# A cross-attention and expert-layer kernel: a new order for the prologue's instructions, 15 identity transposes in its gaps, and a last copy in two pieces

## The chip, the cores and the metric

One core of one Trainium2 chip runs the whole program. The metric is the device time of one launch in microseconds (us), as the median of several runs. "Faster" means less of it.

## What is computed

16 batches of 100 rows of width 256 go through two residual blocks. Cut to what matters:

```python
LN = layernorm                       # over the 256 columns, no weight
# block 1: 16 heads of width 16, keys and values from ctx (16, 361, 256)
Q, K, V = LN(x) @ Wq.T + bq, ctx @ Wk.T + bk, ctx @ Wv.T + bv
p   = softmax(Q K^T / 4)             # per batch and head: 100 x 361
x   = x + tanh(g_xattn) * ((p V) @ Wh.T + bh)
# block 2: 8 experts as low-rank deltas on shared weights, the best 2 per row
t   = rmsnorm(LN(x)) * norm_w
w   = top-2 of softmax(t @ gate_w.T), scaled to sum 1
h1  = t @ w1.T + 2 (t a1_e^T) b1_e^T ;  h3 the same with w3, a3, b3
o_e = (silu(h1) h3) @ w2.T + 2 (...) ;  x = x + tanh(g_ffn) * sum_e w_e o_e
```

## The kernel before

All five engines run one hand-written instruction list each, and semaphores tie them together. A wait on an engine holds back everything behind it on that engine, so the written order is the schedule. There are four stages.

**The prologue** (0 to 44.18 us here). TensorE first does 34 transposes of the 128x128 identity, which depend on nothing but `ident`. Then, for four chunks c of four batches each, the rows are normalized, turned and projected to queries; keys and values of batches 0 and 1 are made; and the 16 score heads of batch 0 are run for their row maxima. The steps, with their function and line:

- `stat`, `spread_of` (L786 to L795), `shift_of` (L799): mean and variance of the batches, on VectorE; `rooted` (L538): the root, on ScalarE.
- `normed` (ScalarE, L533): four batches of one chunk normalized into `xn`. `normed(2)` is batches 8 to 11, `normed(3)` batches 12 to 15.
- `turn(n)` (TensorE, L1216): batches 2n and 2n+1 transposed; `turned(n)` (ScalarE, L475) copies them out of PSUM into `xnT`.
- `q_proj(c, j)` (TensorE, L1227): half j of the queries of chunk c, in bank 2 or 3. `q_high` (ScalarE, L484) and `q_low` (VectorE, L809) split it into a high and a low part; after `q_low` the bank is free.
- `k_proj(b, j)` (L1240), then `k_high` (ScalarE, L496) and `k_low` (VectorE, L818); `v_proj(b, t)` (L1252), then `v_out` (ScalarE, L502).
- `s_head(b, h)` (TensorE, L1270): score head h of batch b, in bank 0 or 1 by turns; `head(b, h)` (VectorE, L985) takes its row maxima. A score head waits for the maxima of the head two before it, which leave its bank.
- `row_turn(0, half)` (TensorE, L1276) turns the maxima of eight heads, and `row_copy`, `row_send` (ScalarE, L513, L517) put them beside the queries.

The queries and keys are stacked for the scores by DMA: `kn` to `KS` from SyncE (`k_stack`, L244, high parts) and GpSimd (`k_stack_low`, L343, low parts), and `q_dram` to `QS` from SyncE (L259) and GpSimd (L363 for batch 0, `q_load`, L333 for later ones). GpSimd also computes the low part of the context (`ctx_low`, L328) and loads later contexts (`ctx_load`, L338).

**The attention body** (`body(i)`, from 44.18 us on): for each batch the exponentials and products with V, together with the scores of the next batch and the keys and values of the one after. Before the first `body`, TensorE waits for `q_low` of the last chunk (`pe.wait_ge(m["q_l"], KT * NC + KT)`), since `st_unit` (L1293) writes the same banks 2 and 3.

**The expert stage**: 32 steps over 4 chunks and 8 slices of the inner width.

**The end**: `down_low` (L1514) finishes the two halves of the output of the last chunk in banks 0 and 1; `out_half` copies one by ScalarE (L632) and the other by VectorE (L950, 128x400); `out_turn_last` (L1503, L1507) transposes both, four pieces each; `added` (L955) adds them to `xs`, two batches at a time; SyncE stores them (L304).

Of the kernel before, what the change touches and what calls it, by code (L numbers as in the profile page):

```python
# [21 lines left out]
KT = D // 128  # L22
# [19 lines left out]
def program(nc, x, ctxT, g_x, g_f, wqT, bq, wkT, bk, wvT, bv, whT, bh,  # L42
            norm_w, w1T, w3T, w2T, agT, b1T, b3T, a2T, b2T, out):
    es = ExitStack()
    with es:
# [263 lines left out]
        def _(pool):  # L309
# [9 lines left out]
            def low_w(w):  # L319
                pool.wait_ge(m["wkv_h"], w + 1)  # L320
                nc.gpsimd.tensor_tensor(wkv[:, w, 1], wst[:, w], wkv[:, w, 0].bitcast(F32), ALU.subtract).then_inc(m["wkv_l"], 1)

            def ctx_low(b):
                if b == 1:
                    pool.wait_ge(m["ctx_ha"], 1)
                else:
                    pool.wait_ge(m["ctx_h"], b if b else 1)
                nc.gpsimd.tensor_tensor(cth[:, b % 2, 1], craw[:, b % 2], cth[:, b % 2, 0].bitcast(F32), ALU.subtract).then_inc(m["ctx_l"], 1)  # L328
# [7 lines left out]
            def ctx_load(b):  # L336
                wait(pool, "ctx_l", b - 1)
                pool.dma_start(craw[:, b % 2, :, 0:T], ctxT[b]).then_inc(ctx_sw[b % 2], 16)  # L338

            def k_stack_low(b):  # L340
                pool.wait_ge(m["dve_kl"], KT * b + KT)
                for g in range(4):
                    pool.dma_start(KS[b % 3][64:96, g, :, :].rearrange("p j t -> p (j t)").bitcast(F32),  # L343
                                   kn[32 * g:32 * g + 32, b % 2, 1, :, :].rearrange("p j t -> p (j t)").bitcast(F32)).then_inc(klst[b % 3][g], 16)

# [10 lines left out]
            ctx_low(0)  # L356
            low_w(0)
            low_w(1)
            pool.wait_ge(m["zero"], 3)
            pool.wait_ge(q_first, 32)  # L360
            src = q_dram[1].rearrange("(g o p) c s -> o p g c s", g=4, o=2)
            for odd in range(2):
                pool.dma_start(QS[0][32 + DH * odd:32 + DH * odd + DH, :, odd, :, :].rearrange("p g j s -> p g (j s)").bitcast(F32),  # L363
                               src[odd][:, :, 0, 0:KT * S]).then_inc(qst[0], 16)
            k_stack_low(0)
            ctx_low(1)
            ctx_load(2)

            def body(i):
# [81 lines left out]
        def _(act):  # L451
# [21 lines left out]
            def turned(n):  # L473
                act.wait_ge(m["xnT_t"], n + 1)
                nc.scalar.activation(xnT[:, :, 2 * n * S:2 * (n + 1) * S].rearrange("p k (b s) -> p b k s", b=2),  # L475
                                     (pT[2], pO)[n % 2][:, 0:2 * KT * S].rearrange("p (b k s) -> p b k s", b=2, k=KT),
                                     ACT.Copy).then_inc(m["xnT_ok"], 1)

            def q_high(c, j):
                act.wait_ge(m["q_mm"], c * KT + j + 1)  # L480
                wait(act, q_out[c % 2], 32 * (c // 2))
                if c == 2:
                    act.wait_ge(q_first, 32)
                nc.scalar.activation(qn[:, c % 2, 0, :, j, :], pT[j][:, 0:CS].rearrange("p (b s) -> p b s", b=4), ACT.Identity, bias=bqs[:, j:j + 1]).then_inc(m["q_h"], 1)  # L484
# [6 lines left out]
            def k_high(b, j):  # L491
                act.wait_ge(m["pe_k"], KT * b + j + 1)
                if j == 0 and b > 1:
                    for g in range(4):
                        wait(act, kst[(b - 2) % 3][g], stacked(32, b - 2, (b - 2) % 3))
                nc.scalar.activation(kn[:, b % 2, 0, j, :], pP[(1, 0)[j]][:, 0:TP], ACT.Identity,  # L496
                                     bias=bks[:, j:j + 1]).then_inc(m["act_kh"], 1)

            def v_out(b, t):
                bank = (pS[0], pS[1], pT[2])[t] if b == 0 else pP[1] if b == 1 and t == 1 else pP[0]  # L500
                act.wait_ge(m["pe_v"], NT * b + t + 1)
                nc.scalar.activation(va[0:TW[t], b % 3, t, :, 0:DH],  # L502
                                     bank[0:TW[t], 0:D].rearrange("p (h d) -> p h d", h=H),
                                     ACT.Copy).then_inc(m["act_v"], 1)
# [20 lines left out]
                nc.scalar.activation(pt[0:TW[t], u, :], pT[u % 3][0:TW[t], 0:CS], ACT.Exp,  # L525
                                     scale=float(DH) ** -0.5).then_inc(m["act_e"], 1)

            def normed(c):
                act.wait_ge(m["xnT_t"], 2 * c - 2)
                act.wait_ge(m["nmr_ok"], 3)  # L530
                act.wait_ge(m["xn_ok"], 6)
                for b in range(4 * c, 4 * c + 4):
                    nc.scalar.activation(xn[:, b % 8, :], xs[:, b, :], ACT.Identity, bias=nmr[:, b:b + 1],  # L533
                                         scale=rstd[:, b:b + 1]).then_inc(m["xn_ok"], 1)

# [26 lines left out]
            q_high(1, 1)  # L562
            rooted(2, 8, B)
            k_high(1, 0)
            k_high(1, 1)
            normed(2)
            turned(4)
            turned(5)
            q_high(2, 0)
            row_out(0, 0)  # L570
            q_high(2, 1)
            v_out(1, 0)
            normed(3)
            v_out(1, 1)
            turned(6)
            turned(7)
            nc.scalar.activation(warm_e[:], nmr[:, 0:1], ACT.Exp).then_inc(m["exp_ok"], 1)
            q_high(3, 0)
            q_high(3, 1)
# [187 lines left out]
        def _(dve):  # L767
# [211 lines left out]
            def head(b, h):  # L979
                n = b * H + h  # L980
                dve.wait_ge(m["pe_s"], n + 1)
                if h % 8 == 0:
                    wait(dve, "pe_cT", 2 * b - 1 + h // 8)
                pos = h // 4 * 4 + h % 2 * 2 + h % 4 // 2
                nc.vector.tensor_reduce(nmax[:, h // 8, pos % 8:pos % 8 + 1], pS[h % 2][0:S, 0:T], AX.X, ALU.max, negate=True).then_inc(m["dve_s"], 1)  # L985
# [24 lines left out]
            stat(2)  # L1010
            stat(3)
            q_low(1, 0)
            q_low(1, 1)
            head(0, 0)
            head(0, 1)
            spread_of(2, 8, B)
            head(0, 2)
            head(0, 3)
            shift_of(2, 8, B)
            k_low(1, 0)  # L1020
            head(0, 4)
            head(0, 5)
            k_low(1, 1)
            head(0, 6)
            head(0, 7)
            q_low(2, 0)
            head(0, 8)
            q_low(2, 1)
            head(0, 9)
            ctx_high(2)  # L1030
            head(0, 10)
            head(0, 11)
            head(0, 12)
            q_low(3, 0)
            head(0, 13)
            q_low(3, 1)
            head(0, 14)
            head(0, 15)

            def body(i):  # L1040
                b = i + 2
# [152 lines left out]
            dve.wait_ge(m["d_zt"], 2 * NC)  # L1194
            dve.wait_ge(m["pe_b2"], 2 * (NC - 1))
            nc.vector.tensor_tensor(zm[:], zt[:, 0], zt[:, 1], ALU.add).then_inc(m["d_zm"], 1)
            out_half(NC - 1)
            added(NC - 1, 0)
            added(NC - 1, 1)

# [2 lines left out]
        def _(pe):  # L1203
# [80 lines left out]
            def st_unit(b, u):  # L1284
                n = b * UN + u
                q, t = u // NT, u % NT
                if u == 0:
                    wait(pe, "cr_a", 16 * (b + 1))
                if u == UN // 2:
                    wait(pe, "cr_b", 16 * (b + 1))  # L1290
                wait(pe, "act_e", n - 2)
                for j in range(KT):
                    last = mm(pT[u % 3][0:TW[t], j * 2 * S:(j + 1) * 2 * S],  # L1293
                              KS[b % 3][:, q, j, T0[t]:T0[t] + TW[t]],
                              QS[b % 3][:, q, :, j, :], start=True, stop=True)
                last.then_inc(m["pe_st"], 1)
# [202 lines left out]
            def out_turn_last():  # L1499
                pe.wait_ge(m["d_wb"], 2 * NC)  # L1500
                pe.wait_ge(m["a_fo"], NC)
                for k in range(4):
                    nc.tensor.transpose(ps[6 + k // 2][0:S, k % 2 * D:k % 2 * D + 128], fo[:, 0, k * S:(k + 1) * S], ident[:])  # L1503
                pe.wait_ge(m["d_fo"], NC)
                for k in range(4):
                    col = k % 2 * D + 128
                    last = nc.tensor.transpose(ps[6 + k // 2][0:S, col:col + 128], fo[:, 1, k * S:(k + 1) * S], ident[:])  # L1507
                    if k % 2:
                        last.then_inc(m["pe_out"], 1)
# [6 lines left out]
            def out_turn(c):  # L1516
# [3 lines left out]
                for k in range(4):  # L1520
# [3 lines left out]
                    if k % 2:  # L1524
                        last.then_inc(m["pe_out"], 1)

            for _ in range(34):
                nc.tensor.transpose(pP[0][:, 0:128], ident[:], ident[:])
            turn(0)
# [14 lines left out]
            s_head(0, 1)  # L1544
            pe.wait_ge(m["dve_kl"], 1)
            k_proj(1, 0)
            s_head(0, 2)
            s_head(0, 3)
            pe.wait_ge(m["dve_kl"], 2)
            k_proj(1, 1)  # L1550
            s_head(0, 4)
            s_head(0, 5)
            s_head(0, 6)
            turn(4)
            turn(5)
            s_head(0, 7)
            q_proj(2, 0)
            s_head(0, 8)
            pe.wait_ge(m["dve_kl"], 3)
# [3 lines left out]
            pe.wait_ge(m["dve_kl"], 4)  # L1563
            v_proj(1, 0)
            s_head(0, 10)
            s_head(0, 11)
            pe.wait_ge(m["act_c"], 1)
            v_proj(1, 1)
            s_head(0, 12)
            turn(6)  # L1570
            turn(7)
            q_proj(3, 0)
            s_head(0, 13)
            q_proj(3, 1)
# [3 lines left out]
            s_head(0, 15)  # L1578
            pe.wait_ge(ones_in, 32)
            pe.wait_ge(m["xnT_ok"], 2 * NC)  # L1580
            pe.wait_ge(m["q_l"], KT * NC + KT)

            def body(i):
                b = i + 2
# [221 lines left out]
```

## Time and profile before

| what | value |
|---|---|
| median of 3 runs | 499.56 us (498.75 to 500.44) |
| the profiled execution, its own time | 499.88 us |
| span of its instructions | 498.0 us |
| TensorE busy | 482.1 us (97%) |
| VectorE, ScalarE, GpSimd busy | 358.4, 265.7, 276.9 us |
| mean granted TensorE clock | 0.995 |

### The profile page before, as it was taken

The numbers are of one execution on the slowest core, as the hardware profiler recorded it, in microseconds if no ns is written. First come the engines' busy times: TensorE is split into PE (matmuls) and PEld (weight loads), VectorE is DVE, ScalarE is ACT, GpSimd is POOL, SyncE is SP. The second block draws the span as 40 slices with busy tenths as digits, with TensorE's granted clock in tenths as the row PEclk, the third lists the DMA queues.
The fourth block names the chain that finished last, engine by engine and source line by source line (L and its number), as shares of the span: only waits on it lengthen the run. The fifth ranks groups of instructions, "written<-read, shape, count | busy, mean of one in ns | idle before, by whom it ended". The sixth has DMA issues, their size and how long they took to land.

```text
span 498.0 us, 11753 instructions
## 1 busy us (share of the span) xinstructions
PE 482.1 (97%) x4350; PEld 454.2 (91%) x4350; DVE 358.4 (72%) x771; ACT 265.7 (53%) x584; POOL 276.9 (56%) x336
## 2 busy tenths in 40 slices
PE   7888999999999999999999999999999999999996
PEld 6657999999999999998999998899999999999994
DVE  5866787888888888988797779745585566764444
ACT  4466766666777766669865532533325333333331
POOL 6545665666666677685434547544485435845440
PEclk9989999999999999999999999999999999999999
DMA  7693786678777676554260000010000100001001
GB/s 214 176 291 98 219 208 163 153 183 195 199 184 180 174 188 158 121 111 79 50 185 1 1 0 2 1 34 1 0 2 0 34 1 1 0 2 34 0 1 33
DMA packets 51144, 45.83 MB, mean 92 GB/s; under 512 B 33935, under 2 KB 40115, under 8 KB 51088
## 3 DMA queue, kind: packets, MB, share of 16 engines
q1 hardware_dynamic: 41310, 23.18, 19.8%
q0 software_dynamic: 7504, 18.69, 14.0%
q10 hardware_dynamic: 2274, 3.21, 2.0%
q8 instruction: 35, 0.57, 0.5%
q14 instruction: 21, 0.17, 0.1%
HBM read 20.59 MB, written 6.66 MB: 55 GB/s over the span
## 4 chain that ended last, share of the span: by engine, by line
PE 90%; DVE 5%; DMA 2%; issue 1%; ACT 1%; SPq 0%; DVEq 0%; ACTq 0%
PE bank L1426 14%; PE bank L1270 9%; PE bank L1293 8%; PE bank L1306 7%; PE bank L1430 7%; PE bank L1443 7%; PE bank L1478 6%; PE bank L1252 6%; PE bank L1240 6%; PE bank L1458 4%; PE bank L1339 3%; PE bank L1461 2%; PE bank L1227 2%; DMA xs<-x 2%; PE bank L1386 2%; PE bank L1318 1%
## 5 line engine op out<-in xcount | busy, mean ns | idle before, releaser
L985 DVE TENSOR_REDUCE nmax<-bank 100x1 f32<-100x361 f32 x256 | 131.1, 530 | 34.0 <-PE bank L1270 29.7
L419 POOL TENSOR_TENSOR awl<-hb,awh 128x400 fp32r<-128x400 f32 x63 | 71.4, 1134 | 119.5 <-ACT awh L623 119.5
L623 ACT ACTIVATE awh<-hb 128x400 fp32r<-128x400 f32 x64 | 34.5, 538 | 118.4 <-DVE hb L921 118.1
L525 ACT ACTIVATE pt<-bank 120x400 f32<-120x400 f32 (+1 forms) x192 | 90.1, 501 | 12.6 <-PE bank L1293 9.5
L1270 PE MATMUL bank<-KS,QS 96*100 96x362 f32 x256 | 86.3, 357 | 3.7 <-DVE nmax L985 2.9
L914 DVE TENSOR_TENSOR hb<-sil,bank 128x400 f32<-128x400 f32 x64 | 36.4, 569 | 71.2 <-PE bank L1443 36.7
L1293 PE MATMUL bank<-QS,KS 97*120 97x200 f32 (+1 forms) x384 | 63.6, 269 | 0.0
L328 POOL TENSOR_TENSOR cth<-craw,cth 128x724 fp32r<-128x724 f32 x16 | 27.7, 1730 | 59.9 <-ACT cth L471 53.6
L1293 PEld LDWEIGHTS bank<-QS,KS 97*120 97x120 f32 (+1 forms) x384 | 59.2, 184 | 0.2
L1270 PEld LDWEIGHTS bank<-KS,QS 96*100 96x100 f32 x256 | 41.6, 167 | 9.6 <-DVE nmax L985 3.3
L333 POOL DMA_DIRECT2D QS<-q_dram x90 | 46.1, 521 | 0.4 <-issue 0.3
L1252 PE MATMUL bank<-wkv,cth 128*120 128x256 f32 (+1 forms) x288 | 45.2, 286 | 0.0
L921 DVE TENSOR_TENSOR hb<-hb,wbT 128x400 f32<-128x400 f32 x64 | 43.4, 678 | 2.1
L1240 PE MATMUL bank<-cth,wkv 128*128 128x362 f32 x192 | 42.0, 331 | 0.0
L343 POOL DMA_DIRECT2D KS<-kn x64 | 31.9, 508 | 15.1 <-DVE kn L818 9.7
L618 ACT ACTIVATE sil<-bank 128x400 f32<-128x400 f32 x64 | 31.6, 493 | 16.3 <-PE bank L1430 11.7
L1252 PEld LDWEIGHTS bank<-wkv,cth 128*120 128x120 f32 (+1 forms) x288 | 39.3, 183 | 0.3 <-issue 0.3
L1306 PE MATMUL bank<-pt,va 120*17 120x100 f32 (+1 forms) x1536 | 36.5, 249 | 0.0
L1306 PEld LDWEIGHTS bank<-pt,va 120*17 120x17 f32 (+1 forms) x1536 | 32.5, 97 | 3.9 <-issue 3.6
L423 POOL TENSOR_TENSOR awsl<-aws,awsh 128x400 fp32r<-128x400 f32 x31 | 34.0, 1097 | 0.0
L1240 PEld LDWEIGHTS bank<-cth,wkv 128*128 128x128 f32 x192 | 32.7, 190 | 0.3
L513 ACT ACTIVATE crow<-bank 8x100 fp32r<-8x100 f32 x32 | 7.7, 242 | 31.4 <-PE bank L1276 31.4
(225 smaller groups left out, 1117.1 us busy)
## 6 DMA issues: line engine op xcount, KB each, us to landing
KS<-kn SPq DMA_DIRECT2D x128, 90.5 KB, 3.3
KS<-kn POOLq DMA_DIRECT2D x64, 90.5 KB, 3.5
craw<-ctxT POOLq DMA_DIRECT2D x14, 361.0 KB, 5.0
QS<-q_dram POOLq DMA_DIRECT2D x92, 50.0 KB, 3.3
q_dram<-qn ACTq DMA_DIRECT2D x4, 400.0 KB, 4.4
o_dram<-on SPq DMA_DIRECT2D x16, 100.0 KB
xr<-o_dram SPq DMA_DIRECT2D x16, 100.0 KB
y<-xs SPq DMA_DIRECT2D x8, 200.0 KB
```

Of the source, the lines that this page charges most:

```text
L333: pool.dma_start(QS[b % 3][row + DH * odd:row + DH * odd + DH, :, odd, :, :].rearrange("p g j s -> p g (j s)").bitcast(F32), src[odd]).the ...
L419: nc.gpsimd.tensor_tensor(awl[:, g % 2, slot], hb[:, slot], awh[:, g % 2, slot].bitcast(F32), ALU.subtract).then_inc(m["p_awl"], 1)
L525: nc.scalar.activation(pt[0:TW[t], u, :], pT[u % 3][0:TW[t], 0:CS], ACT.Exp, scale=float(DH) ** -0.5).then_inc(m["act_e"], 1)
L914: nc.vector.tensor_tensor(hb[:, slot], sil[:, slot], pU[1][:, 0:CS], ALU.mult).then_inc(m["d_hb"], 1)
L921: nc.vector.tensor_tensor(hb[:, slot], hb[:, slot], wbT[g // FT % 2][:, slot], ALU.mult).then_inc(m["d_aw"], 1)
L985: nc.vector.tensor_reduce(nmax[:, h // 8, pos % 8:pos % 8 + 1], pS[h % 2][0:S, 0:T], AX.X, ALU.max, negate=True).then_inc(m["dve_s"], 1)
L1240: last = mm(pP[(1, 0)[j]][:, 0:TP], wkv[:, 0, hw, k, j * 128:(j + 1) * 128], cth[:, b % 2, hc, k, :], start=p == 0, stop=p == 5)
L1252: last = mm(bank[0:TW[t], 0:D], cth[:, b % 2, hc, k, T0[t]:T0[t] + TW[t]], wkv[:, 1, hw, k, :], start=p == 0, stop=p == 5)
L1270: mm(pS[h % 2][0:S, 0:TP], QS[b % 3][0:96, g, h % 2, j, :], KS[b % 3][0:96, g, j, :], start=True, stop=True).then_inc(m["pe_s"], 1)
L1293: last = mm(pT[u % 3][0:TW[t], j * 2 * S:(j + 1) * 2 * S], KS[b % 3][:, q, j, T0[t]:T0[t] + TW[t]], QS[b % 3][:, q, :, j, :], start=True, ...
L1306: last = mm(pO[32 * g:32 * g + VW, q * S:(q + 1) * S], va[0:TW[t], b % 3, t, 4 * q + g, :], pt[0:TW[t], u, g * S:(g + 1) * S], start=t == ...
L1426: mm(pU[a][:, 0:CS], up_w[a][hw][:, j, fs], tt[hc][c % 2][:, j, :], start=t + j == 0, stop=False)
```

## The change

On TensorE, 15 further transposes of the identity into bank 2 are placed in the prologue, in groups of 2, 4, 2, 2, 2 and 3, each group behind a wait for `q_low(1, *)` (`keep_warm`). `turn(4)` stands before score head 6 instead of behind it and `turn(5)` behind head 7 instead of before it; `turn(6)`, `turn(7)` go from behind head 12 to ahead of `v_proj(1, 1)`, and head 11 goes behind that. The wait for the last `q_low` leaves the end of the prologue and is split over the first two `st_unit`. On VectorE, `head(0, 0)` goes ahead of `q_low(1, 1)`, `shift_of(2, ...)` ahead of `head(0, 3)`, `k_low(1, 1)` behind `head(0, 6)`, `ctx_high(2)` behind `head(0, 12)`, and the two `q_low(3, *)` one and two heads later. On ScalarE, `normed(2)` comes before `k_high(1, 1)`, three of the four steps of `normed(3)` before `q_high(2, 0)` and the fourth before `v_out(1, 0)`, and `v_out(1, 1)` behind `turned(7)`. On GpSimd, two of the four `k_stack_low(0)` transfers go ahead of the query load, the other two behind `ctx_low(1)`. At the end, VectorE's copy is made in two pieces of 200 columns, and the transposes wait for one piece each.

```diff
@@ gpsimd @@
+            k_stack_low(0, 0, 2)
             pool.wait_ge(m["zero"], 3)
             pool.wait_ge(q_first, 32)
...
-            k_stack_low(0)
             ctx_low(1)
+            k_stack_low(0, 2, 4)
             ctx_load(2)
@@ scalar @@
             k_high(1, 0)
+            normed(2, 0, 4)
             k_high(1, 1)
-            normed(2)
             turned(4)
             turned(5)
+            normed(3, 0, 3)
             q_high(2, 0)
             row_out(0, 0)
             q_high(2, 1)
+            normed(3, 3, 4)
             v_out(1, 0)
-            normed(3)
-            v_out(1, 1)
             turned(6)
             turned(7)
+            v_out(1, 1)
@@ vector @@
             q_low(1, 0)
+            head(0, 0)
             q_low(1, 1)
-            head(0, 0)
             head(0, 1)
             spread_of(2, 8, B)
             head(0, 2)
+            shift_of(2, 8, B)
             head(0, 3)
-            shift_of(2, 8, B)
...
             dve.wait_ge(m["pe_b2"], 2 * (NC - 1))
             nc.vector.tensor_tensor(zm[:], zt[:, 0], zt[:, 1], ALU.add).then_inc(m["d_zm"], 1)
-            out_half(NC - 1)
+            dve.wait_ge(m["pe_b2"], 2 * NC)
+            for pair in range(2):
+                cs = slice(pair * 2 * S, (pair + 1) * 2 * S)
+                nc.vector.tensor_copy(fo[:, 1, cs], pY[1][:, cs]).then_inc(m["d_fo"], 1)
@@ tensor, st_unit @@
+                if b == 0 and u < KT:
+                    pe.wait_ge(m["q_l"], KT * NC + KT - 1 + u)
@@ tensor, out_turn_last @@
-                pe.wait_ge(m["d_fo"], NC)
                 for k in range(4):
+                    if k % 2 == 0:
+                        pe.wait_ge(m["d_fo"], NC + k // 2)
@@ tensor, prologue @@
+            def keep_warm(n):
+                pe.wait_ge(m["q_l"], 3 * KT)
+                for _ in range(n):
+                    nc.tensor.transpose(pT[0][:, 0:128], ident[:], ident[:])
...
             pe.wait_ge(ones_in, 32)
             pe.wait_ge(m["xnT_ok"], 2 * NC)
-            pe.wait_ge(m["q_l"], KT * NC + KT)
```

TensorE, from score head 4 of batch 0 (bank 0) to the first projection of chunk 2 (bank 2 from `xnT,wq`); before:

```order
L1270 MATMUL bank0<-KS0,QS0 100x362
L1270 MATMUL bank1<-KS0,QS0 100x362
L1270 MATMUL bank0<-KS0,QS0 100x362
L1216 MATMUL bank4<-ident,xn 128x100 x4
L1216 MATMUL bank5<-ident,xn 128x100 x4
L1270 MATMUL bank1<-KS0,QS0 100x362
L1227 MATMUL bank2<-xnT,wq 128x400 x2
```

The same place in the changed kernel, whose lines are some numbers further down:

```order
L1275 MATMUL bank0<-KS0,QS0 100x362
L1538 MATMUL bank2<-ident 128x128 x4
L1275 MATMUL bank1<-KS0,QS0 100x362
L1538 MATMUL bank2<-ident 128x128 x2
L1221 MATMUL bank4<-ident,xn 128x100 x4
L1275 MATMUL bank0<-KS0,QS0 100x362
L1538 MATMUL bank2<-ident 128x128 x2
L1275 MATMUL bank1<-KS0,QS0 100x362
L1538 MATMUL bank2<-ident 128x128 x2
L1221 MATMUL bank5<-ident,xn 128x100 x4
L1538 MATMUL bank2<-ident 128x128 x3
L1232 MATMUL bank2<-xnT,wq 128x400 x2
```

Thirteen of the 15 identity transposes stand here, and the turn into bank 4 has gone ahead of a score head; the work between the first and the last row is otherwise the same.

TensorE again, from the first value projection of batch 1 (bank 6) to the first projection of chunk 3; before:

```order
L1252 MATMUL bank6<-wkv,cth 121x256 x6
L1270 MATMUL bank0<-KS0,QS0 100x362
L1270 MATMUL bank1<-KS0,QS0 100x362
L1252 MATMUL bank7<-wkv,cth 120x256 x6
L1270 MATMUL bank0<-KS0,QS0 100x362
L1216 MATMUL bank4<-ident,xn 128x100 x4
L1216 MATMUL bank5<-ident,xn 128x100 x4
L1227 MATMUL bank2<-xnT,wq 128x400 x2
```

and in the changed kernel:

```order
L1257 MATMUL bank6<-wkv,cth 121x256 x6
L1275 MATMUL bank0<-KS0,QS0 100x362
L1221 MATMUL bank4<-ident,xn 128x100 x4
L1221 MATMUL bank5<-ident,xn 128x100 x4
L1257 MATMUL bank7<-wkv,cth 120x256 x6
L1275 MATMUL bank1<-KS0,QS0 100x362
L1275 MATMUL bank0<-KS0,QS0 100x362
L1232 MATMUL bank2<-xnT,wq 128x400 x2
```

Both turns moved up by a value projection and two score heads; head 11 (bank 1) now has the turns and the projection ahead of it.

VectorE, from head 12 to head 15 of batch 0 and head 0 of batch 1 (the last two `TENSOR_REDUCE`); before:

```order
L985 TENSOR_REDUCE nmax<-bank0 100x1
L809 SCALAR_TENSOR_TENSOR qn<-bank2,bqs,qn 128x4x100
L985 TENSOR_REDUCE nmax<-bank1 100x1
L809 SCALAR_TENSOR_TENSOR qn<-bank3,bqs,qn 128x4x100
L985 TENSOR_REDUCE nmax<-bank0 100x1
L985 TENSOR_REDUCE nmax<-bank1 100x1
L985 TENSOR_REDUCE nmax<-bank0 100x1
```

and in the changed kernel:

```order
L987 TENSOR_REDUCE nmax<-bank0 100x1
L781 CAST cth<-craw 128x724
L987 TENSOR_REDUCE nmax<-bank1 100x1
L811 SCALAR_TENSOR_TENSOR qn<-bank2,bqs,qn 128x4x100
L987 TENSOR_REDUCE nmax<-bank0 100x1
L987 TENSOR_REDUCE nmax<-bank1 100x1
L811 SCALAR_TENSOR_TENSOR qn<-bank3,bqs,qn 128x4x100
L987 TENSOR_REDUCE nmax<-bank0 100x1
```

Each `q_low` of chunk 3 moved down past one or two heads, the second past all that is left of batch 0, and the cast of context 2 now stands behind head 12.

## Rows read from the trace of the kernel before

**Rows 1.** Busy time by stretch: from:to, length, engines in order, granted clock, DMA share, GB/s.

```profile
7.20:10.00 2.80, 0.94 (x9) 0.78 (x9) 1.44 (x4) 2.27 (x6) 1.05 (x1) 1.00 0.92 282
...
25.60:29.00 3.40, 2.22 (x13) 1.38 (x12) 2.95 (x8) 3.14 (x8) 0.56 (x2) 1.00 1.02 338
29.00:32.40 3.40, 2.92 (x6) 1.48 (x6) 0.53 (x1) 0.48 (x1) 3.40 (x7) 0.50 1.04 372
...
44.20:490.00 445.80, 443.91 (x4161) 426.56 (x4162) 327.02 (x683) 242.44 (x537) 248.75 (x292) 1.00 0.33 81
```

**Rows 2.** The chain of waits, 26 to 45 us: start, length (us), what.

```profile
26.37 1.97 ACT xn L533 x4
...
29.58 3.00 PE bank L1227 x4
32.58 0.17 PE bank L1270
32.75 0.09 PE bank L1276
32.84 1.38 PE bank L1227 x4
...
36.02 0.41 PE bank L1270
36.43 0.72 PE bank L1252 x6
...
37.38 0.71 PE bank L1216 x8
38.09 0.67 issue
38.76 1.58 PE bank L1227 x4
...
44.18 0.25 PE bank L1276
```

**Rows 3.** Instructions in order of time: start, length, engine, line, idle before it.

```profile
17.66 1.21 POOL L363 DMA_DIRECT2D QS<-q_dram  x2 [4.53 <-DMA q_dram<-qn]
18.86 2.00 POOL L343 DMA_DIRECT2D KS<-kn  x4
...
22.77 0.55 PE L1270 MATMUL bank<-KS,QS 96*100 96x362 f32 x2 [0.72 <-DMA KS<-kn]
...
28.98 0.50 ACT L475 ACTIVATE xnT<-bank 128x400 f32<-128x400 f32 x1 [0.26 <-PE bank L1216]
...
34.92 0.33 PE L1270 MATMUL bank<-KS,QS 96*100 96x362 f32 x1
...
42.57 0.33 PE L1270 MATMUL bank<-KS,QS 96*100 96x362 f32 x1
```

**Rows 4.** The opening transposes (L1528) alone, by stretch: length, TensorE, weight loads.

```profile
1.50:2.50 1.00, 0.97 (x5) 0.97 (x6) 1.00 0.48 76
...
6.00:6.50 0.50, 0.50 (x7) 0.50 (x6) 1.00 0.84 256
```

**Rows 5.** VectorE's groups by shape, 12 to 24 us: count, busy us, mean ns, idle.

```profile
L809 DVE SCALAR_TENSOR_TENSOR qn<-bank,bqs,qn 128x400 fp32r<-128x400 f32 x2 | 1.3, 634 | 1.5 <-ACT qn L484 1.5
...
L985 DVE TENSOR_REDUCE nmax<-bank 100x1 f32<-100x361 f32 x2 | 1.0, 524 | 0.0
L809 DVE SCALAR_TENSOR_TENSOR qn<-bank,bqs,qn 128x100 fp32r<-128x100 f32 x2 | 0.6, 300 | 0.0
```

**Rows 6.** ScalarE's groups by shape, 12 to 44 us.

```profile
L484 ACT ACTIVATE qn<-bank,bqs 128x400 fp32r<-128x400 f32 x8 | 4.8, 595 | 8.4 <-PE bank L1227 8.4
```

**Rows 7.** The last query load for batch 1 (L333), issued at 33.0 us.

```profile
DMA to landing us min/median/max: 5.0/5.0/5.0
```

**Rows 8.** The end, in order of time, columns as in rows 3.

```profile
492.26 0.57 DVE L950 COPY fo<-bank 128x400 f32<-128x400 f32 x1 [1.70 <-PE bank L1514]
...
493.36 1.41 DVE L955 SCALAR_TENSOR_TENSOR xs<-bank,tgf,xs 100x512 f32<-100x512 f32 x2 [0.52 <-PE bank L1507]
```

More of the change, by code:

```diff
@@ L338, in ctx_load, with k_stack_low @@
                 pool.dma_start(craw[:, b % 2, :, 0:T], ctxT[b]).then_inc(ctx_sw[b % 2], 16)
-            def k_stack_low(b):
+            def k_stack_low(b, g0=0, g1=4):
                 pool.wait_ge(m["dve_kl"], KT * b + KT)
-                for g in range(4):
+                for g in range(g0, g1):
                     pool.dma_start(KS[b % 3][64:96, g, :, :].rearrange("p j t -> p (j t)").bitcast(F32),
@@ L526, in expo, with normed @@
                                      scale=float(DH) ** -0.5).then_inc(m["act_e"], 1)
-            def normed(c):
+            def normed(c, k0, k1):
                 act.wait_ge(m["xnT_t"], 2 * c - 2)
@@ L531, in normed @@
                 act.wait_ge(m["xn_ok"], 6)
-                for b in range(4 * c, 4 * c + 4):
+                for b in range(4 * c + k0, 4 * c + k1):
                     nc.scalar.activation(xn[:, b % 8, :], xs[:, b, :], ACT.Identity, bias=nmr[:, b:b + 1],
@@ L1022, in _ @@
             head(0, 5)
+            head(0, 6)
             k_low(1, 1)
-            head(0, 6)
             head(0, 7)
@@ L1029, in _ @@
             head(0, 9)
-            ctx_high(2)
             head(0, 10)
@@ L1033, in _ @@
             head(0, 12)
+            ctx_high(2)
+            head(0, 13)
             q_low(3, 0)
-            head(0, 13)
-            q_low(3, 1)
             head(0, 14)
             head(0, 15)
+            q_low(3, 1)
             def body(i):
@@ L1546, in _ @@
             k_proj(1, 0)
+            keep_warm(2)
             s_head(0, 2)
@@ L1551, in _ @@
             s_head(0, 4)
+            keep_warm(4)
             s_head(0, 5)
+            keep_warm(2)
+            turn(4)
             s_head(0, 6)
-            turn(4)
+            keep_warm(2)
+            s_head(0, 7)
+            keep_warm(2)
             turn(5)
-            s_head(0, 7)
+            keep_warm(3)
             q_proj(2, 0)
@@ L1565, in _ @@
             s_head(0, 10)
-            s_head(0, 11)
+            turn(6)
+            turn(7)
             pe.wait_ge(m["act_c"], 1)
             v_proj(1, 1)
+            s_head(0, 11)
             s_head(0, 12)
-            turn(6)
-            turn(7)
             q_proj(3, 0)
```

## The prediction

> **What bounds the kernel now.** I read the busy time by stretch first. From 44.20 to 490.00 us TensorE is busy for 443.91 of 445.80 us [rows 1], so whatever lets the attention body start earlier moves all that follows by as much, and only the prologue and the last few microseconds have anything to give. The point to watch is the second `row_turn` of batch 0, at 44.18 us [rows 2]: from there on the order of work is the old one.
>
> The chain of waits shows what the prologue waits for. TensorE is not the cause up to 29.48 us: four normalizations (26.37 us, 1.97 long), then `turn(5)`, then `turned(5)` on ScalarE, which ends at 28.98 + 0.50 = 29.48 [rows 2, 3]. Behind it stand four losses, all on TensorE's path:
>
> - **The clock.** From 29.00 to 32.40 us the granted clock is 0.50, that is 1.2 GHz [rows 1]. `q_proj(2, 0)` takes 3.00 us there, and the same work at 38.76 us takes 1.58 at 2.4 GHz [rows 2]: 1.42 us lost. In the 3.40 us before the fall TensorE was busy for 2.22 [rows 1].
> - **Head 11.** Head 10 ends at 34.92 + 0.33 = 35.25 [rows 3]. Head 11 waits for the maxima of head 9, which stand behind `q_low(2, 1)` on VectorE, and ends at 36.43 [rows 2]. A head in a dense stream takes 0.17 [rows 2]. Lost: 36.43 - 35.25 - 0.17 = 1.01 us.
> - **`q_proj(3, 0)`.** `turn(7)` ends at 38.09; the projection waits for `turned(7)` and ends at 38.76 + 1.58 = 40.34 [rows 2]. Without a gap it takes 1.38, as `q_proj(2, 1)` does [rows 2]. Lost: 40.34 - 38.09 - 1.38 = 0.87 us.
> - **The last heads.** Head 15 ends at 42.57 + 0.33 = 42.90 [rows 3], and the `row_turn` comes 1.28 us later, since head 14's maxima stand behind `q_low(3, 1)`.
>
> **The change, part by part.**
>
> *Up to 29.5 us: 0.* The first score head started after 0.72 us of idling for a `KS` transfer that GpSimd issued at 18.86, behind two query loads. GpSimd had idled for 4.53 us before these [rows 3], so two key transfers (a half of the 2.00) fit there and the query loads are not held up. The head may start some 0.7 us earlier, but the chain goes through ScalarE, not through it. There `normed(2)` begins one `k_high` earlier, and that `k_high` then stands ahead of `turned(4)`; the two cancel, and `q_proj(2, 0)` starts at 29.5 again. What this makes late: the keys of batch 1 leave two microseconds later on SyncE and one later on GpSimd (rival 3).
>
> *The identity transposes: their own cost 0, the clock -1.4.* At the end of the opening run 7 of them take 0.50 us [rows 4], 0.071 each, so 15 take 1.07. Thirteen fall between heads 4 and `q_proj(2, 0)`, 13 x 0.071 = 0.92, in gaps in which TensorE waits for maxima and normalizations: 3.40 - 2.22 = 1.18 us are idle there [rows 1]. If a gap were gone, the group in it would cost at most 4 x 0.07 = 0.3. They raise the busy time of that stretch from 2.22 to about 3.1 of 3.40. I take the full 1.42 as gained. Against: between 7.20 and 10.00 TensorE was busy for only 0.94 of 2.80 and the clock stayed at 1.00 [rows 1], so busy time alone does not tell when it falls. Bounds: 0 and 1.42.
>
> Do such transposes count as work for the clock at all? At the start nothing else ran on TensorE: 5 of them in the first microsecond, then 7 in a half [rows 4], and the pace more than doubled. I read this as the clock rising on transposes alone, though the column of the granted clock says 1.00 throughout. The Trainium skill says the opposite ("TensorE: Matmul & The Clock Gate", Part 4: PE-mode transpose): transposes do not count as work in the same way, and the full clock does not engage for them. By that rule the 15 do nothing and the sum below is smaller by its clock term. The trace speaks against the rule, so it is a rival and not the forecast.
>
> *The order behind 29.5 us: -2.6.* TensorE's list now has `turn(6)`, `turn(7)` and `v_proj(1, 1)` ahead of head 11. I lay it out densely. `q_proj(2, 0)`, head 8, `row_turn` and `q_proj(2, 1)`: 29.5 + 1.58 + 0.17 + 0.09 + 1.38 = 32.72. Then up to head 15 seven heads (7 x 0.17), three value projections (3 x 0.72), two turns (0.71) and two query projections (2 x 1.38): 6.82, which makes 39.54 [rows 2]. Is any of it held? Head 12 needs the maxima of head 10: 32.72 plus `q_high` 0.60, `q_low` 0.63 and two maxima of 0.52 is 35.0 [rows 5, 6], and TensorE comes there at 35.4. `q_proj(3, 0)` needs `turned(7)`, which has a value projection and two heads to run beside, 1.06 us, more than the 0.67 it was waited for [rows 2]. So the losses of 1.01 and 0.87 go. At the end, `q_low(3, 1)` stands behind head 15 and TensorE no longer waits for it before `row_turn`; what is left is the maxima of head 15, 0.52 and some hundredths, so 1.28 becomes 0.56 and -0.72 comes out. The `row_turn` falls at 39.54 + 0.56 = 40.1 instead of 44.18: -4.08, of which 1.42 is the clock and -2.66 the order (1.01 + 0.87 + 0.72 and 0.06 of rounding). Against it: `q_low(3, 1)`, 0.63, now stands ahead of the maxima of head 0 of batch 1, for which head 2 waits. They end 0.63 + 0.52 = 1.15 behind `row_turn`, where head 2 would be issued at about 1.0: +0.15. Together -3.95. Lower bound of the order's part: if head 11's hold and the one at the end come back whole in other places, -0.8; upper bound -2.66.
>
> *The copy in two pieces: -0.25.* It takes 0.57 for 400 columns [rows 8]. `q_low` at 400 and 100 columns takes 634 and 300 ns [rows 5], 1.11 ns a column, so 200 columns fewer save 0.22 and a piece takes 0.35. The transposes of the first pair start that much earlier, the second piece (0.35) runs beside them, and `added` for the second pair follows the first as before. Gain 0.2 to 0.25; the loss can be no more than the second fixed cost, 0.57 - 0.44 = 0.13, if nothing overlaps. -0.2 here.
>
> **The sum.** 0 - 3.95 - 0.2 = -4.15, against the profiled execution's 499.88: 495.7 us. That execution lies 0.3 above the median of the runs, which have a spread of 1.7; I give 495.6.
>
> **Rivals.**
>
> *1. The clock falls all the same* (or in another place of the prologue). For it: the idle stretch at 7.20 without a fall [rows 1] shows that the clock does not simply follow the busy time of a stretch, so 0.92 us more of it need not hold it. Against: the pace of the opening transposes [rows 4]. It gives back 1.42: 495.7 + 1.42 = 497.1 us. The Trainium skill's rule on transposes, above, would end here too.
>
> *2. The waits only move.* TensorE's dense stream of 10 us behind 29.5 needs VectorE and ScalarE on time at every head; the nearest margin is 0.4 us (head 12). If two or three of the heads are late by half a microsecond each, 1.0 to 1.5 come back, with the clock held: 495.7 + 1.2 = 496.9; with rival 1 as well, 498.3.
>
> *3. The stacks of batch 1 become the bound; slower.* The place is head 0 of batch 1, at about 39.5 now. GpSimd's last query load for it was issued at 33.0 and took 5.0 us [rows 7], so it landed at 38.0, well ahead of its use behind 42.90. Now it is issued 0.9 later (it stands behind `k_stack_low(1)`, which waits for the moved `k_low(1, 1)`) and lands at 38.9. From 39.5 on each microsecond of landing costs one. It cancels the gain of 4.15 only where the load needs 33.9 to 43.7, 9.8 us instead of 5, and is slower by over 1.5 from some 11.3 us. For it: the DMA share is 1.02 and 1.04 from 25.60 to 32.40 [rows 1], and the transfers of `KS` now start later in a full queue. Against: the bytes are the same, and a delay of 1 us cannot make them twice as slow. At 11.3 us: 495.7 + (33.9 + 11.3 - 39.5) = 501.4.
>
> *4. Nothing of size changes*, because the shift is absorbed by a wait early in the body, such as one for maxima behind the added `q_low(3, 1)`; only the end's 0.2 is left: 499.6. Against: the body's busy time above.
>
> **Chances.** Forecast 0.55; rival 1 0.20; rival 2 0.14; rival 3 0.04; rival 4 0.07. A measurement here tells 0.3%, 1.5 us, from no change, so "faster" is below 498.1. Forecast, rival 1 and most of rival 2 lie there: 0.83. Same: the rest of rival 2 and rival 4, 0.12. Slower: 0.05. The range has to leave out 2 in 10 at most: its low end is the sum less half the spread of the runs (0.85), 494.8; its high end takes in rival 1, rival 2 and nearly both together, 498.2.
>
> **What would show it.** Right: granted clock 1.00 in all slices of the prologue; `q_proj(2, 0)` at 29.5 taking about 1.6; head 11 directly behind `v_proj(1, 1)`; no gap ahead of `q_proj(3, 0)`; the `row_turn` of batch 0's second half at about 40.1; `added` 0.2 earlier against its copy's start. Wrong: a clock of 0.50 anywhere behind 7 us, idle time of TensorE of over half a microsecond between 30 and 39 us, a wait of head 0 of batch 1 for a DMA, or a body longer than before between that `row_turn` and the end.

## The result and the profile after

| | before | changed |
|---|---|---|
| median of 4 runs | 500.00 us (498.75 to 500.63) | 494.79 us (494.68 to 496.00) |
| ratio, 95% interval | | 0.9906 (0.9880 to 0.9931) |
| the profiled execution | 499.88 us | 494.78 us |
| its span | 498.0 us | 493.0 us |
| second `row_turn` of batch 0 | 44.18 us | 39.52 us |

In a later series, beside the experiments below, the changed kernel had a median of 496.75 us over 10 runs and before 499.74 over 26: ratio 0.9930 (0.9904 to 0.9957). The change makes the kernel faster by 0.7 to 0.9%.

The same changed kernel is thus 2.0 us slower in the later series. Of the 1.9 us between the spans of the two profiled executions (494.9 and 493.0), 0.58 lie ahead of the second `row_turn` and 1.3 behind it. Behind it TensorE waited for two transfers in the later one, for which it did not wait in the first one, nor in the profiled execution of before:

```profile
PE bank L1337 <- DMA xr<-o_dram: 0.7, 1, 0.7
PE bank L1300 <- DMA QS<-crow: 0.2, 1, 0.2
```

Whether the new order makes such waits more frequent is open: there is one trace of the kernel before. What else slows the later series is not known either; its runs had no more falls of the clock than the first.

The chain of waits of the changed kernel, 19 to 40 us (start, length, what), answers to [rows 2]:

```profile
2.08 9.92 DMA xs<-x
...
19.12 2.92 PE bank L1232 x8
...
28.57 0.31 issue
28.88 1.58 PE bank L1232 x4
30.46 0.16 PE bank L1275
30.62 0.09 PE bank L1281
30.71 1.37 PE bank L1232 x4
...
33.14 0.70 PE bank L1221 x8
33.84 0.73 PE bank L1257 x6
34.57 0.33 PE bank L1275 x2
34.90 1.35 PE bank L1232 x4
...
38.84 0.55 DVE nmax L987
39.38 0.14 issue
39.52 0.25 PE bank L1281
```

From 28.88 to 38.81 us the chain is TensorE's own list without a gap. The projection of chunk 2 takes 1.58 us, heads 11 and 12 follow the value projection directly (0.33 us for the two), and the projection of chunk 3 starts with no wait.

Its busy time by stretch, the same columns as [rows 1]:

```profile
25.60:29.00 3.40, 3.09 (x26) 2.59 (x25) 3.18 (x7) 3.40 (x8) 0.18 (x1) 1.00 0.98 358
29.00:32.40 3.40, 3.40 (x14) 2.14 (x15) 1.08 (x2) 2.23 (x6) 3.40 (x8) 1.00 0.98 335
...
40.20:485.90 445.70, 443.70 (x4160) 426.16 (x4158) 327.16 (x683) 242.17 (x536) 252.55 (x299) 1.00 0.34 82
```

The clock stays at 1.00, that is 2.4 GHz, and the body behind is as dense as it was. The span shrank by 5.0 us: 4.66 by the `row_turn`, 0.22 by the copy at the end (below), and the last 0.1 in between, where single waits differ from execution to execution.

### The profile page after: what moved, and what is told of

Read it like the earlier page. It is cut to its first block, busy times and chain, and to the rows that moved or that the text cites. A ratio compares the mean times of both kernels' runs of the same rounds, so it can differ in the third digit from the quotient of the medians.

```text
span 493.0 us, 11786 instructions
## 1 busy us (share of the span) xinstructions
PE 482.1 (98%) x4365; PEld 456.1 (93%) x4365; DVE 358.6 (73%) x772; ACT 265.5 (54%) x584; POOL 277.0 (56%) x336
## 4 chain that ended last, share of the span: by engine, by line
PE 92%; DVE 4%; DMA 2%; issue 1%; SPq 0%; DVEq 0%; ACT 0%
PE bank L1433 14%; PE bank L1275 9%; PE bank L1300 8%; PE bank L1313 7%; PE bank L1437 7%; PE bank L1450 7%; PE bank L1257 7%; PE bank L1485 6%; PE bank L1245 6%; PE bank L1465 4%; PE bank L1346 3%; PE bank L1468 2%; DMA xs<-x 2%; PE bank L1393 2%; PE bank L1232 2%; PE bank L1325 1%
## 5 line engine op out<-in xcount | busy, mean ns | idle before, releaser
L333 POOL DMA_DIRECT2D QS<-q_dram x90 | 46.1, 521 | 0.4 <-issue 0.2
```

The lines of the kernel that those rows point to most:

```text
L333: pool.dma_start(QS[b % 3][row + DH * odd:row + DH * odd + DH, :, odd, :, :].rearrange("p g j s -> p g (j s)").bitcast(F32), src[odd]).the ...
```

## How the experiments are read

Executions differ ahead of the part in question. The first transfers land at other times: in some the chain starts with the rows (`DMA xs<-x`, as above), in others with the first context, and then the query projections of chunk 1 end up to 1.3 us later; in three (no opening transposes, turns late, a step further) it starts with a fill of `KS` by VectorE. So positions are counted from the end of these eight records, the **anchor** (19.12 + 2.92 = 22.04 above). "Stream" is the start of the first projection of chunk 2, "turn" the second `row_turn` of batch 0.

| kernel | anchor | to stream | stream to turn | anchor to turn |
|---|---|---|---|---|
| before | 22.06 | 7.52 | 14.60 | 22.12 |
| changed | 22.04 | 6.84 | 10.64 | 17.48 |
| changed, again | 22.63 | 6.82 | 10.65 | 17.47 |
| no transposes | 22.74 | 6.89 | 10.63 | 17.52 |
| no transposes, again | 23.17 | 7.12 | 10.63 | 17.75 |
| transposes alone | 22.06 | 7.53 | 13.17 | 20.70 |
| late half alone | 22.57 | 7.70 | 12.31 | 20.01 |
| no opening transposes | 24.31 | 6.83 | 10.63 | 17.46 |
| turns late | 22.18 | 6.83 | 12.55 | 19.38 |
| GpSimd as before | 22.93 | 7.33 | 10.64 | 17.97 |
| ScalarE as before | 22.79 | 7.26 | 10.64 | 17.90 |
| last wait as before | 22.04 | 6.82 | 11.21 | 18.03 |

An anchor-to-stream time can differ by 0.2 us without a cause in the edit: it is 6.89 and 7.12 in two executions of the kernel without transposes.

Each run also lists its mean granted clock. A fall of 3.4 us to half costs 0.0034 of it over this span, so I count runs with 0.996 or less as runs with a fall. The count is not sharp at 0.997: a fall alone would read 0.9966, and so can a run without one, since the granted clock also drops behind TensorE's last work (the profiled execution of "ScalarE as before" reads 0.997 with 1.00 in all of the prologue, and 0.64 from 490 us on). The runs were taken in series, each on another chip, and the fall is not equally frequent in them, so only kernels of one series are compared:

| series | before | late half alone, no transposes | changed, without the 15 transposes | kernels with the 15 transposes |
|---|---|---|---|---|
| first: the clock, turns late | 15 of 21 | | 0 of 4 | 0 of 26 |
| second: GpSimd, ScalarE, last wait, a step further | 6 of 7 | | | 0 of 7 |
| later: the kernels taken again, late half alone, one copy | 10 of 26 | 6 of 12 | 3 of 11 | 0 of 11 |

With the four runs of the result, the nine kernels that have the 15 transposes come to 0 of 48, against 31 of 54 of before. Five of the 48 stand at 0.997, and the trace of one of the five has no fall; the other four can't be told.

## Experiments on the clock

**The 15 transposes taken out.**

```diff
             def keep_warm(n):
                 pe.wait_ge(m["q_l"], 3 * KT)
-                for _ in range(n):
-                    nc.tensor.transpose(pT[0][:, 0:128], ident[:], ident[:])
```

> The changed kernel without the 15 identity transposes, everything else in its new order. Theory (the transposes hold the clock, the order alone does not): the granted clock falls to 0.50 for some 3.4 us behind 29 us or nearby, the first projection of chunk 2 takes about 3.0 us instead of 1.58, and the time is 1.4 us above the changed kernel's 494.8, about 496.2. Rival (the new order closes the gaps by itself, the transposes do nothing): clock 1.00 throughout, 494.8.

Measured: 495.70 us (494.77 to 496.56, 4 runs), ratio to before 0.9902 (0.9873 to 0.9931); clock 0.998 or 0.999 in all four. Stream to turn 10.63, as in the changed kernel. By these four runs my theory was wrong. But four are few for an event that also stays out now and then in the kernel before, so I took it again, with more runs of both:

> The changed kernel once more, beside the next ones on the same chip. 494.7 to 495.5, clock 0.998 or more in all runs.

> The changed kernel without its 15 identity transposes, with more runs than the first time, in which the clock had not fallen in any of four. If the new order alone holds the clock: 0.997 or more in all runs and within 0.3 us of the changed kernel. If the transposes hold it and the four were luck: 0.994 to 0.996 in most runs, as in the kernel before, and 1.4 us more.

Measured: 496.75 us with the transposes (495.25 to 497.79, 10 runs, lowest clock 0.997) and 496.87 without (495.53 to 499.70, 11 runs, of which three at 0.994, 0.994 and 0.995). Neither expectation holds as it stands. The fall does come with the new order alone, in 3 of 11 runs. Whether the order makes it rarer is not shown: beside it before had 10 of 26, which 11 runs can't tell from 3, while the 0 of 4 of the first series, against 15 of 21, speak for it. With the transposes it was 0 of 10 in the later series. That is fewer than in before (10 of 26), but against the 3 of 11 it could be chance too; what shows that the transposes hold the clock is the next experiment. On the median they are worth 0.1 us here, which is less than these runs can tell.

**The transposes alone, in the order of before.** Added: `keep_warm` as in the change, with 2, 4, 2, 2, 2 and 3 transposes behind the same steps in the old list.

> The kernel before with the 15 identity transposes in the same gaps and its old order. Theory: the clock stays at 1.00 between 22 and 44 us, and the second row turn of batch 0 comes 1.4 us earlier than 44.18, at about 42.7; time 1.4 us below that of before, 498.4. Rival (by the rule that transposes do not count for the clock): it falls all the same, no change.

Measured: 499.04 us (498.16 to 499.44, 10 runs), ratio 0.9971 (0.9956 to 0.9986), no fall in ten runs, beside 15 in the 21 of before. In the profiled execution anchor and stream stand as before, and behind the stream this changed:

```profile
29.59 1.58 PE bank L1227 x4
31.17 0.17 PE bank L1270
31.34 0.09 PE bank L1276
31.43 1.38 PE bank L1227 x4
...
42.76 0.25 PE bank L1276
```

The turn comes at 42.76 instead of 44.18, by the 1.42 us that the prediction had for the clock. The median moved by 1.1 (500.14 to 499.04), since before only some runs had anything to win: 15 of 21, and 0.71 x 1.42 = 1.0. This speaks against the rival by which transposes do not count.

**Only the late half of the order, without transposes.** The changed kernel with the old order of GpSimd, ScalarE, VectorE and TensorE up to the first projection of chunk 2 and an empty `keep_warm`:

```diff
-            k_stack_low(0, 0, 2)
...
-            k_stack_low(0, 2, 4)
+            k_stack_low(0)
             ctx_low(1)
...
-            normed(2, 0, 4)
             k_high(1, 1)
+            normed(2, 0, 4)
...
-            turn(4)
             s_head(0, 6)
+            turn(4)
+            turn(5)
             s_head(0, 7)
-            turn(5)
```

> No identity transposes, and the order of before on all engines up to the first projection of chunk 2; only the order behind it is new. If the clock falls after the sparse stretch between 25.6 and 29 us, as in the trace of before, it falls here too: clock near 0.995 in most runs, projection of chunk 2 about 3.0 us, and time 0.7 (first half) + 1.4 (clock) above the changed kernel, about 497.1. If the dense stream behind it prevents the fall: 495.7 and clock 0.998.

Measured: 497.54 us (496.21 to 500.84, 12 runs), ratio 0.9947 (0.9918 to 0.9976); six of twelve with a fall. The profiled execution is one of them. By stretch:

```profile
25.60:29.00 3.40, 2.13 (x12) 1.27 (x11) 3.36 (x9) 3.23 (x8) 0.05 (x1) 1.00 1.02 371
30.00:31.00 1.00, 0.73 (x1) 0.46 (x2) 0.21 (x1) 1.00 (x4) 1.00 (x3) 0.66 1.02 405
31.00:32.00 1.00, 1.00 (x3) 0.64 (x2) 0.00 (x0) 0.49 (x1) 1.00 (x3) 0.50 1.00 311
```

and its chain:

```profile
30.27 2.97 PE bank L1231 x4
...
33.70 1.44 PE bank L1231 x4
```

The clock goes to 0.50 after a stretch in which TensorE was busy for 2.13 of 3.40 us, close to the 2.22 of before [rows 1]. Stream to turn is 12.31 here and 10.64 in the changed kernel: the fall costs 1.67 in this execution, 0.25 more than the 1.42 of before. So the difference of the two with a fall, 14.60 - 12.31 = 2.29, is too small for the late half of the order; the two without one, the transposes alone and the changed kernel, give 13.17 - 10.64 = 2.53. The dense order behind the stream does not prevent the fall: 6 of 12, beside 10 of 26 of before. Whether the new order ahead of the stream does is not shown: 3 of 11 against 6 of 12 can be chance.

**No opening transposes.**

```diff
-            for _ in range(34):
-                nc.tensor.transpose(pP[0][:, 0:128], ident[:], ident[:])
```

> The changed kernel without the 34 identity transposes at its start, the only other place where nothing but transposes runs. If transposes raise the clock, the first projections of chunk 0 behind 9.9 us now run at 1.2 GHz, each matmul record about 0.7 us instead of 0.36, and two to four us of the prologue are lost: 497 to 499. If they do not count, nothing changes: 494.8.

Measured: 498.43 us (497.24 to 500.15, 10 runs), ratio 0.9961 (0.9943 to 0.9980). The first work of TensorE in this kernel, then in the changed one, in order of time:

```profile
8.43 1.57 PE L1221 MATMUL bank<-ident,xn 100*128 100x100 f32 x8 [8.43 <-DVE xn L806]
10.68 4.48 PE L1232 MATMUL bank<-xnT,wq 128*128 128x400 f32 x8 [0.69 <-ACT xnT L476]
```

```profile
8.34 0.92 PE L1221 MATMUL bank<-ident,xn 100*128 100x100 f32 x8
9.98 2.92 PE L1232 MATMUL bank<-xnT,wq 128*128 128x400 f32 x8 [0.72 <-ACT xnT L476]
```

The same eight records take 4.48 us against 2.92, and the eight transposes ahead of them 1.57 against 0.92, though nothing but transposes was taken away. The first of the eight records last 874 ns each and the last 499, which is the median of all eight in the changed kernel: here the clock rises in the middle of them. The anchor comes 2.3 us later, and from it to the turn it takes 17.46 us, against 17.48 in the changed kernel. So identity transposes alone had brought the clock up. The Trainium skill's rule ("TensorE: Matmul & The Clock Gate", Part 4) that they do not count in this way does not hold for the transposes of this kernel; this run and the one with the transposes alone both speak against it.

## Experiments on the order

**Turns 6 and 7 and head 11 back.**

```diff
             s_head(0, 10)
-            turn(6)
-            turn(7)
+            s_head(0, 11)
             pe.wait_ge(m["act_c"], 1)
             v_proj(1, 1)
-            s_head(0, 11)
             s_head(0, 12)
+            turn(6)
+            turn(7)
             q_proj(3, 0)
```

> The changed kernel with TensorE's turns 6 and 7 and head 11 back where they were (heads 10 and 11, value projection, head 12, turns, projection). Theory (two separate holds, each worth what the trace of before shows): head 11 is held by the maxima of head 9 for 0.7 us and the projection of chunk 3 waits for the copy of turn 7 for 0.7 to 0.9 us, so about 1.4 to 1.6 above the changed kernel: 496.3. Rival (the dense stream has slack elsewhere that takes it up): 494.8 to 495.1.

Measured: 497.61 us (497.05 to 498.67, 6 runs), ratio 0.9950 (0.9926 to 0.9975). Both holds are back in the chain:

```profile
33.53 0.45 DVE nmax L987
33.98 0.04 issue
34.02 0.41 PE bank L1275
34.43 0.72 PE bank L1257 x6
35.15 0.17 PE bank L1275
35.32 0.69 PE bank L1221 x8
36.01 0.69 issue
36.70 1.58 PE bank L1232 x4
```

Stream to turn grows by 12.55 - 10.64 = 1.91, which is the 1.01 + 0.87 of the prediction; I had expected a little less here. The dense stream has no slack that takes these up.

**GpSimd's order back.**

```diff
-            k_stack_low(0, 0, 2)
             pool.wait_ge(m["zero"], 3)
...
-            ctx_low(1)
-            k_stack_low(0, 2, 4)
+            k_stack_low(0)
+            ctx_low(1)
```

> The changed kernel with GpSimd's order of before: all four key transfers behind the query loads and ahead of the low part of context 1. Theory (the earlier key transfer is what moved the start of the dense stream, by way of VectorE): score head 0 waits for the transfer until about 22.7 us again, the maxima of head 0 end at 23.7 and the low part of the queries now stands behind them, so the variance step starts 0.9 later than in the changed kernel and the second row turn of batch 0 comes 0.6 to 0.9 later, at 40.1 to 40.4. Rival (my prediction's view: that transfer is off the path): row turn at 39.5 as in the changed kernel.

Measured: 496.78 us, a single run. Anchor to stream 7.33 instead of 6.84: +0.49, less than expected. TensorE waits again ahead of the first head:

```profile
23.21 0.57 PE L1274 MATMUL bank<-KS,QS 96*100 96x362 f32 x2 [0.28 <-DMA QS<-q_dram]
```

but for a query transfer, and for only 0.28 us, since in this execution TensorE itself arrived 0.9 later than in the trace of before. That the order of the key transfers causes the 0.49 is not shown, because the first head can be late or early with either order. In the transposes alone, which have GpSimd's old order, it starts with no wait, 0.48 ahead of the anchor as in the changed kernel:

```profile
21.58 0.80 PE L1270 MATMUL bank<-KS,QS 96*100 96x362 f32 x2
```

and in the second profile without transposes, which has the new one, its weights wait as here for a query transfer and it starts with the anchor:

```profile
23.16 0.25 PEld L1275 LDWEIGHTS bank<-KS,QS 96*100 96x100 f32 x2 [0.64 <-DMA QS<-q_dram]
```

What these traces do show is what the head's start is worth. With VectorE's new order a late first head delays the variance step: anchor to that step is 1.67 us in the changed kernel, 1.87 and 2.16 where the head waits. With the old order an early one gains nothing: the transposes alone have anchor to stream 7.53, before has 7.52.

**ScalarE's key copy back ahead of the normalizations.**

```diff
-            normed(2, 0, 4)
             k_high(1, 1)
+            normed(2, 0, 4)
```

> The changed kernel with the keys of batch 1, second half, copied by ScalarE before the four normalizations again. Theory (behind the normalizations the copy fills the time in which ScalarE would wait for turn 5): the projection of chunk 2 starts 0.3 us later against the start of the variance step, so the row turn comes 0.3 later. Rival (my prediction's view: the two cancel): no difference. If it is worth more, 0.5: the whole copy was on the path.

Measured: 495.82 us, a single run. Anchor to stream 7.26: +0.42, between the 0.3 of the theory and the whole copy. ScalarE's timeline shows what the new place buys:

```profile
28.55 0.49 ACT L476 ACTIVATE xnT<-bank 128x400 f32<-128x400 f32 x1
29.45 0.51 ACT L476 ACTIVATE xnT<-bank 128x400 f32<-128x400 f32 x1 [0.41 <-PE bank L1221]
```

Between the two copies ScalarE idles for 0.41 us, waiting for `turn(5)`. In the changed kernel the key copy lies there, and both copies run without a gap. The 0.42 is more than the new place gained in the change, since in this execution from the start of the variance step to the stream it takes 5.59 us, against 5.43 in before and 5.17 in the changed kernel: `turn(5)` stands behind head 7 and two transposes in the new list (28.90 us here, head 7 at 28.43), so the old place of the copy costs more than it did.

**The last wait back.** `q_low(3, 1)` ahead of heads 14 and 15 on VectorE, and TensorE's wait for it at the end of the prologue.

```diff
             q_low(3, 0)
+            q_low(3, 1)
             head(0, 14)
             head(0, 15)
-            q_low(3, 1)
```

> The changed kernel with the wait for the last low part of the queries back at the end of the prologue and that step back ahead of the maxima of heads 14 and 15. Theory (third hold of the trace before): from the end of head 15 to the row turn it takes 1.28 us instead of 0.71, so the row turn and all behind it come 0.57 later. Rival (the body takes it up, since VectorE has that step behind it either way): row turn later, but the first product with V at the same 49.84.

Measured: 495.17 us, a single run. Stream to turn 11.21: +0.57, as expected to the hundredth. But the first product with V starts at 50.28 against 49.84, +0.44: the body takes back 0.13. I put that down to VectorE, which does the same work either way; it is not shown. Theory and rival each had a share.

**One copy at the end.** The whole of bank 1's output half in one `tensor_copy`, with both increments at once.

> The changed kernel with VectorE's last copy in one piece. Theory (the first pair's transposes start when its own 200 columns are there): from the start of the last products (L1522) to the first sum (L957) it takes 0.2 to 0.25 us more than the 2.53 of the changed kernel. Rival (the second piece's fixed cost eats it): the same.

Measured: 496.36 us, a single run. This kernel, then the changed one:

```profile
487.11 1.63 PE bank L1520 x4
488.82 0.58 DVE fo L1200
...
489.92 0.75 DVE xs L957
```

```profile
485.80 1.61 PE bank L1522 x4
487.43 0.62 PE bank L1510 x4
488.04 0.27 PE bank L1515 x2
...
488.33 0.75 DVE xs L957
```

From the last products to the first sum: 489.92 - 487.11 = 2.81 against 488.33 - 485.80 = 2.53; before it was 493.36 - 490.61 = 2.75. Two pieces are worth 0.22 to 0.28.

**A step further.** On VectorE `q_low(3, 1)` goes between heads 14 and 15; on TensorE the first unit and the first half of the key projection go ahead of the `row_turn`, the second half ahead of head 2 of batch 1.

```diff
-                if i == 0:
-                    second_rows(0)
                 st_unit(i, 0)
+                if i == 0:
+                    pe.wait_ge(m["act_c"], 1)
+                    pe.wait_ge(m["ctx_h"], b)
+                    k_part(b, 0, 0, 3)
+                    second_rows(0)
                 s_head(i + 1, 1)
...
```

> A try to go on: the changed kernel with the last low part of the queries ahead of the maxima of head 15 on VectorE (which idles 0.35 there), and on TensorE the first unit of the body, the first half of the key projection of batch 2 ahead of the row turn and its second half ahead of head 2 of batch 1. If TensorE's gap of 0.7 us ahead of the row turn is the bound: the first product with V 0.5 to 0.7 earlier. If VectorE bounds body 0 (it runs without a gap from 39.3 to 45 us): 0.28 earlier and no more, 494.5.

Measured: 495.41 us (494.53 to 495.84, 4 runs), ratio 0.9909 (0.9887 to 0.9932). In its profiled execution, with the anchor at 22.05, the products with V start here:

```profile
48.53 0.54 DVE nmax L987
49.12 0.41 PE bank L1275
49.52 2.20 PE bank L1313 x96
```

That is 49.52 against 49.84, 0.32 earlier, near the 0.28 for which VectorE is the bound; TensorE again ends the stage waiting for maxima. By the median it can't be told from the changed kernel, so I don't call it better.

## Why the prediction was right, and where it was off

It was right in sign, in place and nearly in size: 495.6 us was forecast and 494.79 measured, at the very low end of the range (and 496.75 in the later series). Between the two profiled executions 4.15 us were forecast and 5.1 came. VectorE's variance step, which the first point below needs, stands here before and here in the changed kernel:

```profile
24.15 0.63 DVE L791 BATCH_NORM_AGGREGATE mv<-stats 100x2 f32<-100x6 f32 x8
23.71 0.63 DVE L793 BATCH_NORM_AGGREGATE mv<-stats 100x2 f32<-100x6 f32 x8
```

By the prediction's steps:

- **"Up to 29.5 us: 0" failed.** The stream started at 28.88, 0.70 earlier, or 0.68 counted from the anchor. From the anchor to the variance step it takes 1.67 instead of 2.09: 0.42. I let the earlier first head save nothing, but VectorE, in its new order, takes the maxima of head 0 in the time in which it had idled ahead of `q_low(1, 1)`. From the step to the stream it takes 5.17 instead of 5.43: 0.26. I took one `k_high` ahead of the normalizations and the same `k_high` behind them as equal; behind them it lies beside the wait for `turn(5)`. The two undone one by one cost 0.49 and 0.42, together more than the 0.68, for the reasons given with them. GpSimd's query loads were held up a little too, which I had ruled out: they leave at 18.03 instead of 17.66.
- **The identity transposes: cost 0, clock 1.42.** Right for an execution with a fall, and shown by the transposes alone (44.18 to 42.76). In the chain each takes 0.11 us and not the 0.071 that I took from the opening run, but they lie in gaps: stream to turn is the same with and without them, and anchor to stream no longer. TensorE was busy for 3.09 of 3.40 us with them, as forecast (3.1). One reading in favour of them was weak: in [rows 4] the pace grows from 5 to 14 a microsecond, and two levels of the clock can make no more than a factor of two of it; what made the rest is not known. The run without the opening transposes shows the rise by itself. What I had missed is that the fall is not there in every execution: 31 of 54 of before, so on the average the term is worth about 0.57 x 1.42 = 0.8 us, and more or less of it by series.
- **The order behind the stream: -2.66.** 2.53 between the two executions without a fall, the transposes alone and the changed kernel. The holds of head 11 and of the projection of chunk 3 gave 1.91 when brought back, against 1.88. The wait at the end left 0.71 instead of 0.56, as the maxima of head 15 start 0.03 behind it, last 0.55 and the turn starts 0.14 after them. The +0.15 for VectorE at the start of the body came as 0.1: the first product with V came 4.56 us earlier, the turn 4.66.
- **The copy: -0.2.** 0.22.

So the forecast of 495.6 owes a part of its closeness to luck. The 0.68 ahead of the stream were not in it, the clock's 1.42 were counted in full against a profiled execution that had a fall, and the same kernel measured 2.0 us more in the later series.

Rival 1, the clock: no fall in 44 of the 48 runs with the transposes, and four can't be told. Rival 2: none of the waits in the stream came back. Rival 3: head 0 of batch 1 ended directly behind head 15, with no wait for a transfer; transfers are waited for further on in the body in the later series (above), for under 1 us. Rival 4: the early body kept 4.56 of the 4.66 us.

## What to carry to other kernels

Where one engine runs a dense body behind a prologue full of short waits, lay the prologue out from the chain of waits: move a step that waits for another engine behind work that is ready, and look at what the other engines do in the time that this opens. Short transposes in the gaps cost nothing here, and with them the fall of TensorE's clock was not seen again; count such a gain by how many executions have the fall, not by the profiled one alone, and compare the counts within one series, since the fall itself was twice as frequent in one as in another (15 of 21 and 10 of 26). Compare single executions from a common point behind the first transfers, since these shift the rest by more than such an edit is worth.

## What I had not expected

- The granted clock differs from run to run of one and the same kernel, and no run here shows why: 31 of 54 runs of before at 0.991 to 0.996, the others at 0.997 to 1.000. Medians of these two groups (up to 0.996, and from 0.998) are 500.42 and 499.11 us.
- The column of the granted clock does not show the level at which TensorE starts. Without the opening transposes it reads 1.00 where the records of 10.68 to 15.16 us run at two thirds of the pace of the changed kernel's.
- The first context's landing moves the whole program by up to 1.3 us: the anchor lies at 22.04 to 22.18 us in some executions and at 22.57 to 23.33 in others (the run without the opening transposes aside). In these the chain starts with a line like this one, of the changed kernel in the later series:

```profile
1.78 7.80 DMA craw<-ctxT
```
